# Attention's routing batches reordered: copies ahead of exponentials, lowests ahead of scatters, context in two buffers

## The reference

```python
# x [8,256,256], ctx [8,77,256], 16 heads of 16
q, k, v = norm(x) @ wq + bq, ctx @ wk + bk, ctx @ wv + bv
s = (q @ k.T / 4) * mask;  s = where(s == 0, -1e9, s)
x = x + tanh(g_xattn) * (softmax(s) @ v @ wo + bo)
# 4 experts, each token goes to its 2 best; h is 1024 wide
logits = norm(x) @ router_w + router_b
gates = softmax over the two best logits
out = sum_e gates[t, e] * (silu(norm(x) @ w1[e]) * (norm(x) @ w3[e])) @ w2[e]
x = x + tanh(g_ffn) * out
```

## Time and profile before

| | |
|---|---|
| median of 3 runs | 528.44 us (528.23 to 528.6) |
| the profiled execution, its own time | 529.63 us |
| its span, first to last instruction | 527.80 us |
| busy, share of the span | PE 93%, PEld 85%, DVE 76%, ACT 58%, POOL 35% |
| mean granted clock of TensorE | 0.963 |

### The profile page before, as it was taken

How to read it: one execution, slowest core, us unless ns; L and a number is a source line. 1 busy time by engine, 2 the same in 40 slices (tenths; PEclk the granted TensorE clock), 3 DMA queues, 4 the chain that set the end, 5 groups by cost and what they waited for, 6 DMA issues and landing times.

```text
span 527.8 us, 11417 instructions
## 1 busy us (share of the span) xinstructions
PE 493.0 (93%) x3630; PEld 446.6 (85%) x3630; DVE 402.8 (76%) x955; ACT 304.9 (58%) x724; POOL 183.2 (35%) x190
## 2 busy tenths in 40 slices
PE   9999999997996999999999999999999999999991
PEld 7556777775775899899999989999999999998880
DVE  2588888994895488888788888888878878887660
ACT  3025556544444466578656665676667667766650
POOL 1445657368648103453024452122112201222111
PEclk9979999996995899999999999999999999999996
DMA  8999883001101311312201321221122102211110
GB/s 272 357 392 392 356 329 129 20 21 52 52 22 49 94 43 42 63 24 62 39 12 32 83 43 41 41 42 21 22 42 41 20 20 30 30 21 21 21 11 11
DMA packets 32392, 45.13 MB, mean 85 GB/s; under 512 B 9709, under 2 KB 28781, under 8 KB 32109
## 3 DMA queue, kind: packets, MB, share of 16 engines
q1 hardware_dynamic: 24807, 34.66, 19.3%
q0 software_dynamic: 6576, 8.92, 10.0%
q10 hardware_dynamic: 960, 0.94, 0.6%
HBM read 33.50 MB, written 21.82 MB: 105 GB/s over the span
## 4 chain that ended last, share of the span: by engine, by line
PE 54%; DVE 24%; issue 7%; ACT 5%; POOL 5%; DVEq 1%; DMA 1%; ACTq 0%; SPq 0%; POOLq 0%
PE ps_scores L1719 16%; PE ps_wide L1739 6%; DVE w_lo L1335 5%; PE ps_misc L1739 5%; PE ps_probT L1719 5%; PE ps_wide L1556 4%; DVE w_lo L1331 3%; DVE hid_lo L1344 2%; DVE ps_scores L1340 2%; PE ps_misc L1501 2%; PE ps_scores L1527 2%; PE ps_misc L1578 2%; PE ps_scores L1768 2%; ACT hid_hi L937 2%; POOL score L1052 2%
## 5 line engine op out<-in xcount | busy, mean ns | idle before, releaser
L1119 POOL DMA_INDIRECT out_x<-y_out,meta x35 | 57.4, 1640 | 207.6 <-DVE y_out L1363 202.5
L1335 DVE TENSOR_TENSOR w_lo<-w,w_hi 128x512 fp32r<-128x512 f32 x152 | 104.1, 686 | 15.4 <-ACT w_hi L916 7.9
L1719 PE MATMUL ps_scores<-xt_hi,w_hi 128*128 128x256 f32 x384 | 110.7, 288 | 0.2 <-DVE xt_lo L1349 0.2
L1719 PE MATMUL ps_scores<-xt_lo,w_hi 128*128 128x256 f32 x384 | 108.6, 283 | 0.0
L1719 PE MATMUL ps_scores<-xt_hi,w_lo 128*128 128x256 f32 x384 | 108.6, 283 | 0.0
L916 ACT CAST w_hi<-w 128x512 fp32r x152 | 95.3, 628 | 3.5 <-issue 3.1
L1719 PEld LDWEIGHTS ps_scores<-xt_hi,w_hi 128*128 128x128 f32 x384 | 73.6, 192 | 0.9 <-DVE xt_lo L1349 0.5
L1719 PEld LDWEIGHTS ps_scores<-xt_lo,w_hi 128*128 128x128 f32 x384 | 73.6, 192 | 0.0
L1719 PEld LDWEIGHTS ps_scores<-xt_hi,w_lo 128*128 128x128 f32 x384 | 73.6, 192 | 0.0
L937 ACT CAST hid_hi<-ps_scores 128x256 fp32r<-128x256 f32 x96 | 35.8, 373 | 57.5 <-DVE ps_scores L1340 56.1
L1052 POOL TENSOR_TENSOR score<-score,lowest 128x616 f32<-128x616 f32 x32 | 38.9, 1217 | 56.1 <-DVE lowest L1210 55.8
(11 more groups left out here) (238 smaller groups left out, 1234.6 us busy)
## 6 DMA issues: line engine op xcount, KB each, us to landing
grouped<-in_pad SPq DMA_DIRECT2D x1, 10296.0 KB
w<-in_L_ffn_w SPq DMA_DIRECT2D x8, 1024.0 KB, 12.4
w2s<-in_L_ffn_w SPq DMA_DIRECT2D x4, 1024.0 KB, 13.7
xg<-grouped SPq DMA_DIRECT2D x16, 256.0 KB, 2.7
out_x<-xall SPq DMA_DIRECT2D x8, 256.0 KB, 2.1
xall<-in_x SPq DMA_DIRECT2D x1, 1024.0 KB, 13.2
xall<-in_x SPq DMA_DIRECT2D x1, 768.0 KB, 7.7
ctxT<-in_ctx_t SPq DMA_DIRECT2D x2, 308.0 KB, 5.4
```

The costliest lines, as they stand in the source:

```text
L1119: pool.indirect_dma_start(out, bass.IndirectOffsetOnAxis(ap=meta[:, s % 2, t, E:E + 1].bitcast(U32), axis=0), y_out[:, s % 2, t, :], None, ...
L1335: dve.tensor_tensor(w_lo[:, f % NB], unit_weights(e, f), w_hi[:, f % NB].bitcast(F32), ALU.subtract).then_inc(w_lo_done, 1)
L1719: mm = pe.matmul(ps_gu[f % NB][:, m, 0:n], lhs, rhs[:, a, c, 0:n], start=(k == 0), stop=(k % (3 * DC) == 3 * DC - 1), skip_group_check=True)
```

## The change

In the batches that route, the order within the four streams is altered.

- **ScalarE.** In a FINAL batch `probT_copy(b, 0)` comes ahead of `exponent(b, 1)`. In a BEGIN batch the order behind it becomes: `q_copy`, `norm2` of two tiles, `ctxT_copy`, copy of piece 0, `probT_copy(b, 1)`, `exponent(b, 2)`, `norm2` of the other two, copy of piece 1, `probT_copy(b, 2)`, `exponent(b, 3)`. The last batch has its own order (`ending`).
- **TensorE.** In a BEGIN batch `turn2(k, 0)` moves from ahead of `turn_ctx` to behind `turn_p(b, 1)`, directly ahead of the wait for its copy; `turn2(k, 1)` moves behind `project_o`. In the last batch the three pieces go into the banks of the scores, and `route_product` is issued in one part, last. Both `fill_gap` are gone.
- **VectorE.** `invert` comes ahead of the zeros of step 0.
- **GpSimd.** In a FINAL batch `gates` and `fill` come ahead of `lower(b, 0)`. In batch 5 two scatters are issued, at its end; six go behind steps 0, 1 and 2 of batch 6. In batch 7 one scatter is ahead of `lower(7, 1)` and seven come behind `lower(7, 3)`.
- **Memory.** `ctxn` has two buffers, by `b % 2`, and `context(b, s)` waits for `turn_ctx` of batch b - 2 in place of b - 1. `blank`, the zeros of the first products, is the tile `one_row`, which is set to ones later.

```diff
# ScalarE
-                    exponent(b, 1, first)
-                    probT_copy(b, 0, first)
+                    if b in FINAL:
+                        probT_copy(b, 0, first)
+                        exponent(b, 1, first)
+                    else:
+                        exponent(b, 1, first)
+                        probT_copy(b, 0, first)
+                    if last:
+                        return
+                    q_copy(b + 1)
                     if b in BEGIN:
                         norm2(act, BEGIN[b], range(0, 2))
-                    ...
+                        ctxT_copy(b - 1)
+                        turned2_copy(act, BEGIN[b], 0)
+                        probT_copy(b, 1, first)
+                        exponent(b, 2, first)
+                        norm2(act, BEGIN[b], range(2, GN))
+                        turned2_copy(act, BEGIN[b], 1)
+                        probT_copy(b, 2, first)
+                        exponent(b, 3, first)
...
+                def ending(b):
+                    k = BEGIN[b]
+                    ctxT_copy(b - 1)
+                    probT_copy(b, 1, False)
+                    exponent(b, 2, False)
+                    norm2(act, k, range(0, 2))
+                    probT_copy(b, 2, False)
+                    exponent(b, 3, False)
+                    turned2_copy(act, k, 0, ps_scores[0][:, 0])
+                    norm2(act, k, range(2, GN))
+                    probT_copy(b, 3, False)
+                    turned2_copy(act, k, 1, ps_scores[0][:, 1])
...
+                weights_hi(0, e, 0)
+                turned2_copy(act, NG - 2, 2, ps_scores[0][:, 0])
# GpSimd
-                    lower(b, 0)
                     if b in FINAL:
                         gates(pool, FINAL[b])
                         fill(pool, FINAL[b])
+                    lower(b, 0)
+                    if b in FINAL:
                         places(pool, FINAL[b])
-                    elif not last:
+                        if last:
+                            scatter(pool, FINAL[b], COPIES[0:1])
+                    else:
+                        if b - 1 in FINAL:
+                            scatter(pool, FINAL[b - 1], COPIES[2:4])
                         keys(b + 1, 0)
                     lower(b, 1)
...
+                    if b - 1 in FINAL:
+                        scatter(pool, FINAL[b - 1], COPIES[4:6])
                     lower(b, 2)
...
+                    if b - 1 in FINAL:
+                        scatter(pool, FINAL[b - 1], COPIES[6:8])
                     lower(b, 3)
                     if not last:
                         keys(b + 1, 1)
                     if b in FINAL:
-                        scatter(pool, FINAL[b], COPIES[4:8])
+                        if last:
+                            scatter(pool, FINAL[b], COPIES[1:8])
+                        else:
+                            bias_add(b + 1)
+                            scatter(pool, FINAL[b], COPIES[0:2])
# VectorE
-                    if after_first(b):
-                        dve.wait_ge(ctxT_done, b)
-                    dve.tensor_tensor(ctxn[:, t, g * HG:(g + 1) * HG, :], ps_av[:, g, :, 0:DH],
+                    if b > 1:
+                        dve.wait_ge(ctxT_done, b - 1)
+                    dve.tensor_tensor(ctxn[:, b % 2, t, g * HG:(g + 1) * HG, :], ps_av[:, g, :, 0:DH],
...
+                        if s == 0 and b in FINAL:
+                            invert(dve, FINAL[b])
# TensorE
                     attend(b, 0, first)
-                    if b in BEGIN:
-                        turn2(pe, BEGIN[b], 0)
                     if not first:
                         turn_ctx(b - 1, last)
                     turn_p(b, 1, first)
-                    if b in BEGIN:
+                    if b in BEGIN and not last:
+                        turn2(pe, BEGIN[b], 0)
                         pe.wait_ge(x2T_copied, len(PIECES) * BEGIN[b] + 1)
                     turn_p_end(b, 1, first)
...
                     if not first:
                         project_o(b - 1)
+                    if b in BEGIN and not last:
+                        turn2(pe, BEGIN[b], 1)
                     turn_p(b, 2, first)
...
-                        fill_gap(pe, FILL["weights"], ps_scores[0][:, 1])
+                        turn2(pe, BEGIN[b], 0, ps_scores[0][:, 0])
                     attend(b, 2, first)
...
-                turn2(pe, NG - 2, 2, ps_scores[0][:, 0])
                 turn_p(B - 1, 3, False)
                 turn_p_end(B - 1, 3, False)
-                route_product(pe, NG - 2, ps_scores[1][:, 0], range(0, 2))
+                turn2(pe, NG - 2, 1, ps_scores[0][:, 1])
                 attend(B - 1, 3, False)
-                route_product(pe, NG - 2, ps_scores[1][:, 0], range(2, GN))
+                turn2(pe, NG - 2, 2, ps_scores[0][:, 0])
                 turn_ctx(B - 1, True)
+                route_product(pe, NG - 2, ps_scores[1][:, 0])
...
                 turn_in(0, 0)
-                fill_gap(pe, FILL["output"], ps_scores[0][:, 1])
                 project_o(B - 1)
```

60 lines of the change are left out of this document (20 added, 40 removed).

## The result

The changed kernel took 520.90 us in the median of four runs (519.18 to 521.45) against 528.34 (526.66 to 528.60) of the kernel before beside it: a ratio of 0.9848, 95% interval 0.9823 to 0.9873. Measured a second time it took 522.88 against 528.60: 0.9896 (0.9864 to 0.9927; one of its six executions took 2607 us and is left out of the ratio; the median of the other five is 522.15). Forecast were 522.3 us.

A forecast was written before the change was run, and what follows sets the result against it. TensorE was taken as the bound, stopped in batch 5 by ScalarE's copy held behind GpSimd's scatters. Terms -6.7 (batch 5), -0.2 (batch 3), +0.8 (end) gave -6.1 us: 528.44 to 522.3, own range 521.5 to 524.5, wider 518.7 to 524.9.

The forecast's parts named there:

- Batch 5: Stop before `turn_p_end(5, 1)` shrinks from 3.04 to 0.7 us and the clock stays at 2.4 GHz: 6.7 us gained.
- Rivals 2 and 4: 2: batch 5 keeps part of its stop, 525.7 us, chance 0.10; 4: low clock into batch 6, slower, 531.3 us, 0.04.
- Batch 3 and batch 4: Batch 3: the 0.59 us stop before `attend(3, 1)` goes, one of about 0.5 comes, 0.2 us gained; batch 4: no term.
- Batch 6: Six scatters moved here fit into GpSimd's time and delay some `lower`: cost 0 us (0 to 0.6).
- Batch 7: The 2.04 us stop before `attend(7, 0)` goes; one of about 2 us comes before `attend(7, 1)`, waiting for `context(7, 0)`.
- The end: End of attention: `xg` comes 1.9 us earlier, but TensorE idles and runs at 1.2 GHz: +0.8 us in all.
- Rival 1: End of attention: the clock is full when `xg` lands, -2.4 in place of +0.8, 519.1 us; chance 0.25.
- Rival 3: The last seven scatters are slower beside VectorE, 4.6 us later at the end, 526.9 us; chance 0.04.

The follow-up runs named there:

- e1: The changed kernel with all of group 0's scatters back in batch 5, two, two and four behind its lowests: 532.80 us, ratio 1.0077.
- e2: The kernel before with only group 0's scatters spread over batches 5 and 6: 524.12 us, ratio 0.9924.
- e5: The changed kernel with the context in one buffer: 521.93 us, ratio 0.9882.
- e3: The changed kernel with group 1's scatters between the lowests of batch 7 again (two, two, four): 522.99 us, ratio 0.9887.
- e8: The changed kernel with `lower(6, 2)` ahead of two of group 0's scatters: 522.33 us, ratio 0.9888.
- r1: The changed kernel, unaltered, run again on a further chip: 522.88 us, ratio 0.9896.
- r2: The changed kernel with only `project_o(7)` ahead of `turn_in(0)`, run again on a further chip: 521.38 us, ratio 0.9859.
- e9: The changed kernel with one group 1 scatter ahead of `lower(7, 3)` and `lower(6, 2)` ahead of two group 0 scatters: 520.99 us, ratio 0.9849.
- e10: e9 with `project_o(7)` ahead of `turn_in(0)` as well: 519.33 us, ratio 0.9820.
- e4: The changed kernel with `project_o(7)` ahead of `turn_in(0)`: 525.21 us, ratio 0.9937.
- e6: The changed kernel with one of group 1's seven last scatters moved into GpSimd's gap ahead of `lower(7, 3)`: 522.34 us, ratio 0.9889.
- e7: e4 with 24 filler products between `project_o(7)` and `turn_in(0)`: 530.67 us, ratio 1.0034.

## Why the forecast held, and where its terms were off

The two medians, 520.90 and, without the execution of 2607, 522.15, are 1.4 and 0.15 us below the forecast 522.3; the first is 0.6 below the forecast's own range of 521.5 to 524.5, the second in it.

**Batch 5: -6.7, measured -7.12.** The mechanism was as put. The stop of 3.04 became 0.57 (forecast 0.7), the clock stayed at 1.00, which alone is 4.2 of the 7.1, and the stop before `turn_x(7)` halved from 0.65 to 0.33, which I hadn't counted. e1 and e2 show the division: the scatters' spread is the cause of 5.9, the rest of the change, by e5 without the second buffer, adds 1.2. All eleven profiles with both have 17.40 to 17.42. Rivals 2 and 4 didn't occur in batch 5. But what I set against them, that stops of up to 0.65 us leave the clock up, doesn't hold in general: in e3 it fell behind stops of 0.55 and 0.63 us in batch 6. e1 shows how slower than before comes about by another way: a stop of 6.24 us whose low clock reaches into batch 6, and 4.5 us more than before in the median.

**Batch 3 and batch 4: -0.2 and 0, measured -0.09 and -0.02.**

**Batch 6: cost 0 (0 to 0.6), measured about 1.1.** This step was mis-sized: TensorE's idle time went from 0.4 us to 1.5. I let scatters delay lowests and looked no further; the cost came through VectorE. On it `order`, an operation on 128x16 elements, took 3.09 us, and the mask behind it started only then, while GpSimd ran two long operations back to back:

```profile
133.19 3.09 DVE L400 TENSOR_TENSOR order<-above 128x16 f32<-128x16 f32 x1
136.21 0.79 DVE L1224 TENSOR_TENSOR score<-ps_scores,maskt 128x616 f32<-128x616 f32 x1
...
133.79 1.22 POOL L1068 TENSOR_TENSOR score<-score,lowest 128x616 f32<-128x616 f32 x1
134.97 1.27 POOL L1062 TENSOR_TENSOR xall<-xall,row_in 128x512 f32<-128x512 f32 x1
```

It ends when `bias_add` does (136.24), and it is so in all nine profiles in which GpSimd's operations stand like this. The two long operations are not the whole of it. `order` began 0.60 us ahead of `lower`, time enough for its 0.18, beside the end of a scatter (132.76 to 133.76). And beside the same pair, with no scatter ahead of it, a VectorE operation did get in between in the kernel before: `equal` ended with `lower`, and only `above` waited for `bias_add`:

```profile
142.17 0.62 DVE L387 TENSOR_TENSOR equal<-logits 128x64 f32<-128x64 f32 x1
142.71 1.31 DVE L388 TENSOR_TENSOR above<-logits 128x64 f32<-128x64 f32 x1
...
141.49 1.22 POOL L1052 TENSOR_TENSOR score<-score,lowest 128x616 f32<-128x616 f32 x1 [2.26 <-DVE lowest L1210]
142.66 1.28 POOL L1046 TENSOR_TENSOR xall<-xall,row_in 128x512 f32<-128x512 f32 x1
```

What holds `order` through the scatter's end and both operations is open. e8 moves `lower(6, 2)` away from there, and `order` is back at 0.18 us, but then `bias_add` is beside the zeros of the next step, which take 2.49 us instead of 0.80:

```profile
135.43 0.18 DVE L400 TENSOR_TENSOR order<-above 128x16 f32<-128x16 f32 x1
...
136.35 2.49 DVE L1230 SCALAR_TENSOR_TENSOR score<-score 128x616 f32<-128x616 f32 x1
...
136.88 1.29 POOL L1062 TENSOR_TENSOR xall<-xall,row_in 128x512 f32<-128x512 f32 x1
```

These zeros, too, began beside a scatter (135.90 to 136.86), 0.53 us ahead of `bias_add`. The wait moved to another victim: my theory for e8 spoke only of the ranking's operations and had not looked at the zeros, and of routing's small operations `each`, at 140.48, took 1.79 us. TensorE's two stops of batch 6 went and two others came, 0.58 and 0.72 us at 145.39 and 148.68. `attend(7, 0)` came only 0.14 us earlier behind `turn_x(7)`, and the last scatter started 36.24 us behind it instead of 36.36: there the rival was right. The Trainium skill, "SBUF — State Buffer", section "Who interferes with whom", has the rule: a VectorE instruction with two inputs in SBUF contends with GpSimd instructions that read SBUF, one blocking the other fully. Both victims are of that form, and the mask, with an input in PSUM, and the reduction take 0.78 to 0.80 us throughout. In these traces the first to begin isn't always the one that gets through: `order` and these zeros had both begun before the GpSimd operation that they then waited for. I had weighed this section for the scatters only, and not for the operations that the spread pushes together.

**Batch 7: a stop of about 2 us before `attend(7, 1)`.** It came as two, 1.81 us before `attend(7, 0)` and 1.02 before `attend(7, 1)`, both behind a context on VectorE. With batch 6's loss this puts the last scatter 36.36 us behind `turn_x(7)`, where the forecast's is 34.8, and `turn_in(0)` 42.61 behind it where it is 41.4: 1.2 later.

**The end: +0.8, measured +0.17.** The place was right: TensorE through, idle 4.64 us, and a clock of 0.50 when `xg` lands. Wrong was where the low stretch begins. I let it start with `turn_in` and run 6.7 us, 2.4 of them over the experts. It begins in the idle time, at 167.2, 1.2 us after TensorE's last work, and ends near 174.1, ahead of the first expert product at 174.33: only `turn_in` (1.11 instead of 0.60) and `project_o` ran in it. In r1 it begins later, at 172.9, 4.4 us into the idle time, lasts 3.4 us and ends ahead of that product (176.71) as well. That is 1.2 us less than forecast, and turn, product and tail took 3.67 instead of 4.3, 0.6 less: +0.8 + 1.2 - 1.2 - 0.6 = +0.2. That the sum came out is in part luck: rows that came 1.2 us late were paid for by a low stretch that ended in time. In r2 it did not: there it lay over the experts for 4.2 us and cost 1.1, near the forecast's 1.2.

**Rival 1, the full clock when `xg` lands,** isn't what the changed kernel does in either profile, but it is real: e9 and e10 do it, e9 with 2.22 us from `turn_in` to the first expert product instead of 3.67. Its mechanism was as written (a stop in batch 7 drops the clock, and it is back in time). e5 did its first half, and then the clock fell again in the wait of 2.09 us. Which course it takes differs between executions with the same stops. **Rival 3,** scatters slowed by VectorE, did not come at the end: seven of 0.97 us in the mean. The prediction's sentence that the trace has a long scatter "only in this one" was a misreading: the first of batch 5, at 119.70 in the profile before, started beside the zeros and took 1.56 us too (and 1.64 less 0.96 is 0.68, not 0.65). Of group 0's scatters, two that start beside the zeros take 1.56 and 1.36 us in the changed kernel; the eight of group 0 together 8.8 us, 8.4 before.

**The sum.** Forecast -6.1 us. By the landmarks it is 7.0 from batch 3 to the first expert product in both profiles, and 0.4 in the experts, where the forecast had a loss of 1.2 by the low clock and nothing else.

## What to carry to other kernels

Take long work of an off-path engine out of the batch where it delays the critical path and put it behind each step's urgent operation: that was worth five times the reordering of the waiting engines, which alone only moved the stop. When work is moved beside another engine, look for operations of both engines with all inputs in SBUF: a tiny VectorE operation can wait for two of GpSimd's in a row. Laying these apart isn't enough; in e8 it only chose another victim. If the clock falls, a stop's price is its length plus half of what TensorE does in the low stretch behind it. So a stop ahead of idle time can be nearly free, as in e5, and one ahead of dense work is dear. Whether it falls differs between executions of one order, so before a gain or a loss at one place is put down to an edit, follow both profiles back to where they first part: in e3 that was ahead of the edit.

## What the runs showed of the hardware

- A VectorE operation of 0.18 us took 3.09 beside the end of a scatter and two GpSimd operations that followed each other without a gap, in nine of nine profiles; without the scatter, in the kernel before, another one got in between the same two (`equal`, 0.62 us).
- A GpSimd scatter that starts beside VectorE's zeros (`scalar_tensor_tensor`, 128x616, in SBUF) takes 1.36 to 1.64 us where 0.96 is usual.
- A low stretch can begin in TensorE's idle time: at 167.2 in the changed kernel, 1.2 us after its last work, and at 172.9 in r1, 4.4 us after it.
- Equal stops do not have equal effects on the clock. Behind the stop of 1.81 us before `attend(7, 0)` it stayed up in the changed kernel, r1, r2, e4, e6 and e8, and fell, 1.5 to 1.8 us behind the stop's end, in e5, e7, e9 and e10. The stops ahead of it don't tell them apart: e8's are e9's, and e5's are the changed kernel's. In e3 it fell behind a stop of 0.63 us that left it up in the others.
- On one of the three chips of the experiments ScalarE's copy started about 3 us after TensorE's transposes for it, at one place of four different kernels, with no releaser in the trace; in three of them VectorE's `rden` behind `attend(7, 2)` was late so too.
